# Layer 0's integer codes turned over as 16 bit halves: bf16 transposes and unsigned 16 bit copies out of PSUM

## Chip, cores, metric

The kernel runs on one core of a Trainium2 chip, as one launch. The metric is device time in microseconds; before the change it was 2154.37 us, the median of three runs (2153.43 to 2154.45). PE is the engine of the matmuls, DVE the vector engine, ACT the scalar engine, POOL the general one, SP the one that issues the loads.

## What is computed

The reference is a stack of four layers over x, 8 sequences ("elements") of 512 tokens and 256 features, with one conditioning row for each element. Layer 0, where the change lies, is a gated recurrent block and an MLP, all of whose linear maps are of one kind:

```
def _act_quant(x):      # each row to integers -128..127
    scale = 127.0 / clip(max(abs(x), axis=-1), 1e-05)
    return clip(round(x * scale), -128, 127) / scale
def _weight_quant(w):   # -1, 0, 1 times the mean magnitude
    scale = 1.0 / clip(mean(abs(w)), 1e-05)
    return clip(round(w * scale), -1, 1) / scale
def _bitlinear(x, w, nw):
    xn = x * rsqrt(mean(x^2) + 1e-08) * nw
    return _act_quant(xn) @ _weight_quant(w).T
```

For each element: `mx = layernorm(x) * (1 + scale) + shift`; i, f, g = three bitlinears of mx (256 to 256, each with its own norm weight); `i = silu(i) * (1 - sigmoid(f))`; a scan `h = f * h + i` over the tokens; `o = rmsnorm(h) * silu(g)`, a bitlinear of o (256 to 256), gated into x; then a layernorm again, a bitlinear 256 to 2048, `silu(gate) * y`, a bitlinear 1024 to 256, gated into x. Layers 1 (a style merge with a feed forward block), 2 (attention) and 3 (a state space block) follow; nothing of them is changed.

## The kernel before

The program has four parts: `setup` (layer 0's weights made ternary, the conditioning), `layers01` (layers 0 and 1 together), `layer2`, `layer3`. The change is in `layers01` alone. There x stays in SBUF as 8 elements of 4 tiles of 128 tokens. Every engine walks a hand-ordered table (`PE_TURN`, `DVE_TURN`, `ACT_TURN`, `POOL_TURN`) in its own order, once for each element; a row (stage, n, ahead) says which element, counted from the running one, the stage works on, so that several elements in different stages are under way at once. The order of an engine never changes; the engines wait on one another by semaphores.

The codes of a bitlinear take this way. ACT multiplies the rows by their scale and adds ROUND = 12582912 = 1.5 * 2^23 (stages `xq`, `xoq`, `xq2`, `hq`): this rounds to an integer and leaves it in the low mantissa bits of the f32 word. The matmul needs the features on the partitions, so PE turns each 128x128 block over against the f32 identity (`turn`, line 100 of the profile) into PSUM, as f32. DVE copies the turned blocks out of PSUM, subtracts ROUND and writes bf16, in which the integers are exact (stages `qT`, `qoT`, `qT2`, `qhT`: lines 1233, 1263, 1304, 1331). PE then multiplies by the ternary weights in bf16.

For one element: `xw` (three scaled copies of mx, 4 tiles of 6 blocks, 768 columns of PSUM over two banks a tile), `xo` (4 tiles of 2 blocks; its buffer is that of `th`), `mx2` (2 turns of 4 blocks) and `h` (8 turns of 4 blocks): 72 blocks. Two more kinds of transposes in layer 0, `fi` (from `th` and `si`) and `o` (from `si`), and layer 1's are real f32 values. Squares are summed by ACT (line 895) with an accumulator; the squared values themselves go to `junk` tiles that nobody reads.

Of the kernel before, what the change touches and what calls it, by code (L numbers as in the profile page):

```python
# [11 lines left out]
P = 128  # L12
ALU = mybir.AluOpType
ACT = mybir.ActivationFunctionType
AX = mybir.AxisListType
F32 = mybir.dt.float32
BF16 = mybir.dt.bfloat16

B, L, D = 8, 512, 256
T = L // P  # L20
KD = D // P
# [4 lines left out]

ROUND = 12582912.0


# [52 lines left out]
def tok(t):  # L82
    return slice(t * P, (t + 1) * P)
# [545 lines left out]
def layers01(nc, io, w, mean, ident, mod0, style1, x_res, x_loaded):  # L629

    H2 = io["c_harmonics"].shape[0]
    with ExitStack() as ctx:
        def sb(name, shape, dt=F32):
            return ctx.enter_context(nc.sbuf_tensor("l0_" + name, shape, dt))

        def sem(name):
            return nc.alloc_semaphore("l0_" + name)
# [43 lines left out]
        ifg_loaded, vectors_loaded, half_ready, halved = sem("ifg_loaded"), sem("vectors_loaded"), sem("half_ready"), sem("halved")  # L681
        norm_loaded, gate_loaded, mlp_loaded, style_loaded = (
# [43 lines left out]

        def two_banks(a):
            return psum[:, a:a + 2, :].rearrange("p a b -> p (a b)")

# [3 lines left out]
        with nc.Block() as block:  # L733
# [42 lines left out]
            def _(pool):  # L776
                gp = nc.gpsimd
# [110 lines left out]
            def _(act):  # L888
                ac = nc.scalar
# [7 lines left out]
                for stage, t, e in steps(ACT_TURN):  # L897
# [17 lines left out]
                    elif stage == "xq":  # L915

                        act.wait_ge(qs_ready.sem, qs_ready.at(e, 1))
                        for j in range(3):
                            last = ac.activation(xw[:, t, j, :], xw[:, t, j, :], ACT.Copy, bias=ROUND, scale=qs[e % 2][:, t, j:j + 1])
                        last.then_inc(xq_ready.sem, 1)  # L920
# [19 lines left out]
                    elif stage == "xoq":  # L940
                        act.wait_ge(qso_ready.sem, qso_ready.at(e, 1))
                        ac.activation(xo[:, t, :], xo[:, t, :], ACT.Copy, bias=ROUND, scale=qso[:, t:t + 1]).then_inc(xoq_ready.sem, 1)
                    elif stage == "ssq2":
# [4 lines left out]
                    elif stage == "xq2":  # L948
                        act.wait_ge(qs2_ready.sem, qs2_ready.at(e, 1))
                        ac.activation(mx2[:, t, :], mx2[:, t, :], ACT.Copy, bias=ROUND, scale=qs2[:, t:t + 1]).then_inc(xq2_ready.sem, 1)  # L950
                    elif stage == "silu":
# [9 lines left out]
                    elif stage == "hq":  # L961
                        act.wait_ge(qsh_ready.sem, qsh_ready.at(e, 1))
                        ac.activation(h[:, t, :], h[:, t, :], ACT.Copy, bias=ROUND, scale=qsh[:, t:t + 1]).then_inc(hq_ready.sem, 1)
                    elif stage == "setup":
# [51 lines left out]
            def _(pe):  # L1016
                for stage, t, e in steps(PE_TURN):
                    if stage == "xq":

                        pe.wait_ge(xq_ready.sem, xq_ready.at(e, t + 1))  # L1020
                        if t:
                            pe.wait_ge(qT_ready.sem, qT_ready.at(e, t))
                            pe.wait_ge(sg_ready.sem, sg_ready.at(e, t))
                        elif e:
                            pe.wait_ge(qoT_ready.sem, qoT_ready.at(e - 1, T))
                        for j in range(3 * KD):
                            last = turn(nc, two_banks(0)[:, tok(j)], xw[:, t, j // KD, tok(j % KD)], ident[:])
                        last.then_inc(turned.sem, 1)
# [26 lines left out]
                    elif stage == "xoq":  # L1055
# [3 lines left out]
                        for k in range(KD):  # L1059
                            last = turn(nc, psum[:, t % 2, tok(k)], xo[:, t, tok(k)], ident[:])  # L1060
                        last.then_inc(xo_turned.sem, 1)
# [5 lines left out]
                    elif stage == "xq2":  # L1067
# [6 lines left out]
                        for i in range(2):  # L1074
                            for k in range(KD):
                                last = turn(nc, psum[:, 4 + t, tok(KD * i + k)], mx2[:, 2 * t + i, tok(k)], ident[:])
                        last.then_inc(turned2.sem, 1)
# [7 lines left out]
                    elif stage == "hq":  # L1085
# [7 lines left out]
                        for k in range(T):  # L1093
                            last = turn(nc, psum[:, 4 + (3 * i + c) % 2, tok(k)], h[:, i, tok(c * T + k)], ident[:])
                        last.then_inc(h_turned.sem, 1)
# [82 lines left out]
            def _(dve):  # L1178
# [14 lines left out]
                for stage, t, e in steps(DVE_TURN):  # L1193
# [35 lines left out]
                    elif stage == "qT":  # L1229
                        dve.wait_ge(turned.sem, turned.at(e, t + 1))  # L1230
                        if e or t >= 2:
                            dve.wait_ge(y_ready.sem, y_ready.at(e, t - 1))
                        V.tensor_scalar(qT[:, t % 2, :, :].rearrange("p a n -> p (a n)"), two_banks(0)[:, 0:3 * D], ROUND, None,
                                        ALU.subtract).then_inc(qT_ready.sem, 1)
# [24 lines left out]
                    elif stage == "qoT":  # L1259
                        dve.wait_ge(xo_turned.sem, xo_turned.at(e, t + 1))  # L1260
                        if e or t >= 2:
                            dve.wait_ge(yo_ready.sem, yo_ready.at(e, t - 1))
                        V.tensor_scalar(qoT[:, t % 2, :, :].rearrange("p a n -> p (a n)"), psum[:, t % 2, 0:D], ROUND, None,
                                        ALU.subtract).then_inc(qoT_ready.sem, 1)
# [35 lines left out]
                    elif stage == "qT2":  # L1300
                        dve.wait_ge(turned2.sem, turned2.at(e, t + 1))
                        if e:
                            dve.wait_ge(up_ready.sem, up_ready.at(e - 1, 2 * T))
                        V.tensor_scalar(qT2[:, 2 * t:2 * t + 2, :, :].rearrange("p i a n -> p (i a n)"), psum[:, 4 + t, :], ROUND, None,
                                        ALU.subtract).then_inc(qT2_ready.sem, 1)
# [20 lines left out]
                    elif stage == "qhT":  # L1326
                        i, c = t // 2, t % 2
                        dve.wait_ge(h_turned.sem, h_turned.at(e, t + 1))
                        if e or i >= 2:
                            dve.wait_ge(y2_ready.sem, y2_ready.at(e, i - 1))  # L1330
                        V.tensor_scalar(qhT[:, i % 2, c * T:(c + 1) * T, :].rearrange("p a n -> p (a n)"), psum[:, 4 + (3 * i + c) % 2, :], ROUND, None,
                                        ALU.subtract).then_inc(qhT_ready.sem, 1)
# [1163 lines left out]
```

## Time and profile before

| | |
|---|---|
| median of 3 runs | 2154.37 us |
| profiled execution | 2156.48 us |
| its span, first to last instruction | 2154.3 us |
| mean granted clock of PE in the span | 0.913 |
| PE busy | 1839.9 us (85%), 8728 instructions |
| PE weight loads | 1104.3 us (51%) |
| DVE busy | 1328.7 us (62%) |
| ACT busy | 1121.0 us (52%) |
| POOL busy | 568.9 us (26%) |
| `layers01`, its first xl to the last f2 | about 92 to 813 us |

The span is of one profiled execution; busy times are sums of instructions, and those of PE overlap, since a matmul starts before the one ahead has ended. The granted clock is a share of PE's full clock, 2.4 GHz; 0.5 is its lower level, 1.2 GHz. Names in the rows leave out buffer numbers, so `l_mx` stands for mx and mx2, `l_small` for all the small vectors. Some matmul records can be missing from a trace.

### The profile page before, as it was taken

The page shows a single profiled execution, that of the slowest core. Times are in us where ns is not written, and L with a number is a line of the kernel's source. Part 1 is how long each engine was busy: PE and PEld are TensorE (multiplying, and loading weights), DVE is VectorE, ACT ScalarE, POOL GpSimd, SP SyncE. Part 2 cuts the span into 40 slices and gives each one's busy share as a digit, 9 for nine tenths or more (in the row PEclk, how much of TensorE's full clock was granted, in tenths as well). Part 3 has the DMA queues.
Part 4 walks back from the last instruction along what each step waited for, and adds up shares of the span by engine and source line. Part 5 has one row for each costly group of instructions (what it writes and reads, how often), then busy time and mean ns, then how long its engine had stood idle before and what let it go on. Part 6 is the DMA issues. An engine that isn't in the chain of part 4 may idle for free. (4 is left out here: it accounts for less than half of the span.)

```text
span 2154.3 us, 26196 instructions
## 1 busy us (share of the span) xinstructions
PE 1839.9 (85%) x8728; PEld 1104.3 (51%) x8744; DVE 1328.7 (62%) x2922; ACT 1121.0 (52%) x2127; POOL 568.9 (26%) x775
## 2 busy tenths in 40 slices
PE   2355779999999996589899999999999856899998
PEld 1133557677766674133454545454544445567666
DVE  5757698878876516668786868677774114332331
ACT  6556588888776521046756575666666400221221
POOL 0256565567445213000010101010101100323322
PEclk9656699999999997589999999999999977999999
DMA  9400000000000003220203021111200020000000
GB/s 373 127 33 8 18 18 1 18 18 14 1 13 11 3 1 98 52 59 5 63 3 64 7 59 26 40 34 32 53 14 3 6 96 1 3 18 10 20 10 20
DMA packets 88312, 78.20 MB, mean 36 GB/s; under 512 B 9969, under 2 KB 82123, under 8 KB 87923
## 3 DMA queue, kind: packets, MB, share of 16 engines
q1 hardware_dynamic: 88080, 76.50, 12.9%
q8 instruction: 71, 1.16, 0.2%
q14 instruction: 63, 0.51, 0.1%
q10 hardware_dynamic: 98, 0.03, 0.0%
HBM read 46.67 MB, written 4.27 MB: 24 GB/s over the span
## 5 line engine op out<-in xcount | busy, mean ns | idle before, releaser
L1896 DVE TENSOR_REDUCE l_small<-l_psum 128x1 f32<-128x512 f32 x512 | 329.5, 684 | 137.2 <-PE l_psum L1843 132.3
L1655 ACT ACTIVATE l_prob<-l_psum 128x512 f32<-128x512 f32 x512 | 286.4, 596 | 230.0 <-PE l_psum L1713 226.7
L1843 PE MATMUL l_psum<-l_kT,l_qT 96*128 96x512 bf16 x512 | 192.2, 412 | 27.1 <-DMA l_kT<-l_early 12.1
L1713 PE MATMUL l_psum<-l_qT,l_kT 99*128 99x512 bf16 x512 | 175.6, 388 | 16.0 <-ACT l_prob L1655 14.3
L1639 POOL TENSOR_TENSOR k_x_res<-k_x_res,l_add 128x256 f32<-128x256 f32 x32 | 23.3, 727 | 469.9 <-DVE l_add L1940 469.9
L1722 PE MATMUL l_psum<-l_prob,l_v 128*32 128x512 f32 x1024 | 138.1, 612 | 0.2
L1843 PEld LDWEIGHTS l_psum<-l_kT,l_qT 96*128 96x128 bf16 x512 | 49.6, 98 | 171.1 <-DVE l_small L1896 117.9
L1787 PE MATMUL l_psum<-l_w,l_gu 128*128 128x256 f32 x512 | 134.8, 392 | 0.7 <-ACT l_gu L1671 0.7
L94 PE MATMUL l_psum<-l_hT,l_w_f 128*128 128x512 f32 x256 | 120.0, 597 | 5.7 <-ACT l_gu L1013 5.7
L94 PE MATMUL l_psum<-l_hT,l_w 128*128 128x512 f32 x256 | 116.8, 606 | 8.6 <-ACT l_hT L2250 8.6
L94 PE MATMUL l_psum<-l_turned_over,l_w 128*128 128x512 f32 x256 | 120.5, 597 | 4.2 <-ACT l_gu L1671 4.2
L1173 PE MATMUL l_psum<-l_w_f,l_gu 128*128 128x256 f32 x512 | 118.0, 379 | 0.8 <-ACT l_gu L1013 0.8
L94 PE MATMUL l_psum<-l_w,l_gu 128*128 128x256 f32 x512 | 111.9, 379 | 0.8 <-ACT l_gu L2254 0.8
L1787 PEld LDWEIGHTS l_psum<-l_w,l_gu 128*128 128x128 f32 x512 | 97.4, 196 | 19.9 <-issue 2.4
L94 PEld LDWEIGHTS l_psum<-l_w,l_gu 128*128 128x128 f32 x512 | 96.7, 190 | 14.4 <-ACT l_gu L2254 1.6
L1713 PEld LDWEIGHTS l_psum<-l_qT,l_kT 99*128 99x128 bf16 x512 | 46.5, 98 | 108.3 <-ACT l_prob L1655 63.0
L1173 PEld LDWEIGHTS l_psum<-l_w_f,l_gu 128*128 128x128 f32 x512 | 94.5, 190 | 13.1 <-ACT l_gu L1013 1.6
L2254 ACT ACTIVATE l_gu<-l_psum,l_b 128x512 f32<-128x512 f32 x64 | 44.0, 688 | 96.2 <-PE l_psum L94 96.2
L2250 ACT ACTIVATE l_hT<-l_psum,l_shift,l_scale 128x512 f32<-128x512 f32 x16 | 11.7, 775 | 156.4 <-PE l_psum L100 156.4
L94 PE MATMUL l_psum<-l_w_qkv,l_xT 128*128 128x512 f32 (+1 forms) x256 | 90.5, 497 | 2.8 <-DVE l_xn L1958 1.9
L94 PEld LDWEIGHTS l_psum<-l_hT,l_w 128*128 128x128 f32 x256 | 48.4, 194 | 66.3 <-issue 55.6
L94 PE MATMUL l_psum<-k_t_wm,l_qT 128*128 128x512 bf16 x240 | 71.0, 404 | 13.1 <-DVE l_h L1311 7.3
(389 smaller groups left out, 3891.5 us busy)
## 6 DMA issues: line engine op xcount, KB each, us to landing
su_raw<-in_L_cond_wa SPq DMA_DIRECT2D x6, 1536.0 KB, 21.9
l_qT<-l_early SPq DMA_DIRECT2D x32, 192.0 KB, 3.6
l_kT<-l_early SPq DMA_DIRECT2D x32, 192.0 KB, 3.3
k_x_res<-in_x SPq DMA_DIRECT2D x1, 4096.0 KB
l_w<-in_L_cond_W SPq DMA_DIRECT2D x4, 1024.0 KB, 12.5
l_qT<-l_early SPq DMA_DIRECT2D x32, 128.0 KB, 3.1
l_kT<-l_early SPq DMA_DIRECT2D x32, 128.0 KB, 3.0
out<-k_x_res SPq DMA_DIRECT2D x8, 512.0 KB, 2.9
```

The costliest lines, as they stand in the source:

```text
L94: last = nc.tensor.matmul(out, w, m, start=(i == 0), stop=(i == len(pairs) - 1), **kw)
L1173: last = pe.matmul(psum[:, 6 + i % 2, 0:D], gu[:, f, tok(i)], w_f2[:, f, :], start=(f == 0), stop=(f == KF - 1))
L1639: pool.tensor_tensor(x_tile(e, n), x_tile(e, n), add2[:], ALU.add).then_inc(x_ready.sem, 1)
L1655: act.activation(prob[:, s % 2, j, :], psum[:, 2 + n % 2, :], ACT.Exp, scale=float(HD) ** -0.5).then_inc(exp_ready.sem, 1)
L1713: pe.matmul(psum[:, 2 + n % 2, :], kT[e % 2][:, head, tok(s % T)], qT[e % 2][:, head, :], start=True, stop=True).then_inc(st_ready.sem, 1)
L1722: last = pe.matmul(psum[j * BLOCK:(j + 1) * BLOCK, 4, :], v[e % 2][:, kt, at:at + BLOCK], prob[:, n % 2, j, :], start=(kt == 0), stop=(kt ...
L1787: last = pe.matmul(psum[:, mlp_bank(e, t), 0:D], gu[:, f, tok(t)], w_2[:, f, :], start=(f == 0), stop=(f == KF - 1))
L1843: pe.matmul(psum[:, n % 2, :], qT[e % 2][0:SROWS, n // T, tok(n % T)], kT[e % 2][0:SROWS, n // T, :], start=True, stop=True).then_inc(s_re ...
L1896: dve.tensor_reduce(mx[:, n % T, n // T:n // T + 1], psum[:, n % 2, :], AX.X, ALU.max).then_inc(max_ready.sem, 1)
L2250: act.activation(dst[:, k, :], psum[:, bank + k, :], ACT.Identity, scale=scale[:, k, bass.ds(nxt, 1)], bias=shift[:, k, bass.ds(nxt, 1)]). ...
L2254: act.activation(gu[:, n, :], psum[:, n % 2, :], ACT.Gelu_apprx_tanh, bias=b_1[:, n:n + 1]).then_inc(gu_ready.sem, 1)
```

## The change

ACT adds ROUND + CODE, with CODE = 16384, in place of ROUND. The word then is 0x4B400000 + 0x4000 + q, whose low half is 16384 + q, between 16256 and 16511. PE turns over only these low halves: `low` takes an f32 tile as bf16, two to a word, and picks the first of each pair, so the weights of the transpose are bf16 at a pitch of 4 bytes; the identity is a bf16 copy, `identb`, which POOL makes once. The output in PSUM is bf16, packed, so a tile of `xw` fills 1536 bytes of one bank and no longer two banks. DVE reads PSUM as unsigned 16 bit integers, subtracts CODE and writes bf16. PE waits for `identb` once, before the first turn. Five junk tiles of the squares become bf16; `junk_h` stays f32. Transposes of `fi`, `o` and layer 1 are not touched.

```
+CODE = 16384.0
-        junk = [sb(f"junk{i}", [P, D]) for i in range(5)]
+        junk = [sb(f"junk{i}", [P, D], BF16) for i in range(5)]
+        identb = sb("identb", [P, P], BF16)
+        def low(a):
+            return a.bitcast(BF16).rearrange("p (n a) -> p n a", a=2)[:, :, 0]
+        def halves(a):
+            return psum[:, a, :].bitcast(BF16)
+        def codes_in(a, n):
+            return psum[:, a, :].bitcast(U16)[:, 0:n]
 POOL, after its memsets and before its table:
+                gp.tensor_copy(identb[:], ident[:]).then_inc(identb_ready, 1)
 ACT xq; xoq, xq2 and hq alike:
-   ac.activation(xw[:, t, j, :], xw[:, t, j, :], ACT.Copy, bias=ROUND, scale=qs[e % 2][:, t, j:j + 1])
+   ac.activation(xw[:, t, j, :], xw[:, t, j, :], ACT.Copy, bias=ROUND + CODE, scale=qs[e % 2][:, t, j:j + 1])
 PE xq, t = 0, e = 0:
+                        else:
+                            pe.wait_ge(identb_ready, 1)
 PE xq; xoq, xq2 and hq alike:
-   last = turn(nc, two_banks(0)[:, tok(j)], xw[:, t, j // KD, tok(j % KD)], ident[:])
+   last = turn(nc, halves(0)[:, tok(j)], low(xw[:, t, j // KD, tok(j % KD)]), identb[:])
 DVE qT; qoT, qT2 and qhT alike:
-   V.tensor_scalar(qT[...], two_banks(0)[:, 0:3 * D], ROUND, None, ALU.subtract)
+   V.tensor_scalar(qT[...], codes_in(0, 3 * D), CODE, None, ALU.subtract)
```

## Rows read from the trace of the kernel before

**Rows 1.** Windows: start:end and length, busy us of each engine (instructions), clock
```profile
112.00:290.00 178.00, 109.84 (x486) 72.76 (x491) 129.60 (x249) 105.07 (x282) 105.99 (x143) 0.66 0.04 13
290.00:740.00 450.00, 429.80 (x2250) 308.65 (x2261) 352.75 (x729) 344.34 (x809) 250.93 (x343) 0.97 0.04 12
740.00:820.00 80.00, 69.96 (x267) 49.19 (x265) 17.43 (x43) 18.86 (x35) 9.34 (x15) 0.93 0.05 14
```

**Rows 2.** Waits of PE, 300 to 720 us: total us, times, longest
```profile
PE l_psum L94 <- ACT l_gu L1013: 5.7, 8, 0.9
PE l_psum L94 <- DVE l_h L1311: 2.4, 6, 0.5
PE l_psum L94 <- DVE l_qT L1233: 1.8, 1, 1.8
...
PE l_psum L94 <- DVE l_qhT L1331: 1.0, 2, 0.8
```

**Rows 3.** Groups of PE's transposes, 290 to 820 us: count, busy us, mean ns
```profile
L100 PE MATMUL l_psum<-k_ident,l_h 128*128 128x128 f32 x216 | 30.5, 274 | 0.8 <-DVE l_add L1337 0.7
...
L100 PE MATMUL l_psum<-k_ident,l_th 128*128 128x128 f32 x88 | 16.9, 273 | 1.4 <-ACT l_th L942 1.4
L100 PE MATMUL l_psum<-k_ident,l_xw 128*128 128x128 f32 x120 | 16.4, 273 | 1.7 <-ACT l_sg L927 1.7
...
L100 PE MATMUL l_psum<-k_ident,l_mx 128*128 128x128 f32 x48 | 7.0, 273 | 0.0
```

**Rows 4.** Timeline of PE: start us, us of the run, instruction, count
```profile
121.16 1.51 PE L100 MATMUL l_psum<-k_ident,l_xw 128*128 128x128 f32 x6 [1.39 <-ACT l_sg L927]
...
126.57 1.51 PE L100 MATMUL l_psum<-k_ident,l_xw 128*128 128x128 f32 x6 [1.39 <-ACT l_sg L927]
...
139.35 0.66 PE L100 MATMUL l_psum<-k_ident,l_th 128*128 128x128 f32 x2
...
438.65 1.89 PE L1173 MATMUL l_psum<-l_w_f,l_gu 128*128 128x256 f32 x8
439.52 0.81 PE L1173 MATMUL l_psum<-l_w_f,l_gu 128*128 128x256 f32 x3
...
442.99 0.82 PE L100 MATMUL l_psum<-k_ident,l_xw 128*128 128x128 f32 x6
```

**Rows 5.** Timeline of PE in the setup and in layer 2, bf16
```profile
27.99 0.89 PE L94 MATMUL su_t<-su_q,su_t_wa 128*128 128x8 bf16 x28
...
1552.19 0.61 PE L100 MATMUL l_psum<-l_identb,l_part 128*96 128x128 bf16 x8
```

**Rows 6.** Layer 2's tile part: count, ns min/median/max, first and last start
```profile
L100 PE MATMUL l_psum<-l_identb,l_part x512: 217/219/342, 848.2 to 1552.6; 128*96 128x128 bf16 x171
```

**Rows 7.** Groups of DVE's copies out of PSUM, whole span
```profile
L1331 DVE TENSOR_SCALAR l_qhT<-l_psum 128x512 bf16<-128x512 f32 x64 | 42.5, 683 | 5.7 <-PE l_psum L100 5.7
L1233 DVE TENSOR_SCALAR l_qT<-l_psum 128x768 bf16<-128x768 f32 x32 | 30.4, 949 | 10.7 <-PE l_psum L100 10.7
...
L1263 DVE TENSOR_SCALAR l_qoT<-l_psum 128x256 bf16<-128x256 f32 x32 | 13.3, 415 | 3.3 <-PE l_psum L100 3.1
L1912 DVE COPY k_max_rows<-l_psum 12x512 bf16<-12x512 bf16 x32 | 12.9, 405 | 11.8 <-PE l_psum L100 11.8
```

**Rows 8.** Waits between PE and DVE, 112 to 290 us
```profile
PE l_psum L94 <- DVE l_qT L1233: 9.0, 6, 2.6
...
DVE l_qT L1233 <- PE l_psum L100: 8.1, 6, 2.7
```

**Rows 9.** Groups of ACT that write values nobody reads, whole span
```profile
L895 ACT ACTIVATE l_junk<-l_mx 128x256 f32<-128x256 f32 x64 | 26.4, 413 | 16.6 <-POOL l_mx L844 9.1 <-POOL l_mx L807 6.5
...
L271 ACT ACTIVATE su_junk<-su_raw 128x256 bf16<-128x256 f32 x1 | 0.4, 417 | 0.0
```

**Rows 10.** Groups of POOL: layer 2's bf16 copy of the identity
```profile
L1617 POOL CAST l_identb<-k_ident 128x128 bf16<-128x128 f32 x1 | 0.3, 289 | 0.0
```

**Rows 11.** Timeline of POOL, its first work on x
```profile
90.71 0.20 POOL L796 TENSOR_SCALAR l_small<-l_small 128x4 f32<-128x4 f32 x1 [1.95 <-DVE l_small L1204]
```

**Rows 12.** Waits of ACT, 300 to 720 us
```profile
ACT l_h L956 <- PE l_psum L94: 22.7, 27, 4.8
```

More of the change, by code:

```diff
@@ L918, in _ @@
                         for j in range(3):
-                            last = ac.activation(xw[:, t, j, :], xw[:, t, j, :], ACT.Copy, bias=ROUND, scale=qs[e % 2][:, t, j:j + 1])
+                            last = ac.activation(xw[:, t, j, :], xw[:, t, j, :], ACT.Copy, bias=ROUND + CODE, scale=qs[e % 2][:, t, j:j + 1])
                         last.then_inc(xq_ready.sem, 1)
@@ L941, in _ @@
                         act.wait_ge(qso_ready.sem, qso_ready.at(e, 1))
-                        ac.activation(xo[:, t, :], xo[:, t, :], ACT.Copy, bias=ROUND, scale=qso[:, t:t + 1]).then_inc(xoq_ready.sem, 1)
+                        ac.activation(xo[:, t, :], xo[:, t, :], ACT.Copy, bias=ROUND + CODE, scale=qso[:, t:t + 1]).then_inc(xoq_ready.sem, 1)
                     elif stage == "ssq2":
@@ L949, in _ @@
                         act.wait_ge(qs2_ready.sem, qs2_ready.at(e, 1))
-                        ac.activation(mx2[:, t, :], mx2[:, t, :], ACT.Copy, bias=ROUND, scale=qs2[:, t:t + 1]).then_inc(xq2_ready.sem, 1)
+                        ac.activation(mx2[:, t, :], mx2[:, t, :], ACT.Copy, bias=ROUND + CODE, scale=qs2[:, t:t + 1]).then_inc(xq2_ready.sem, 1)
                     elif stage == "silu":
@@ L962, in _ @@
                         act.wait_ge(qsh_ready.sem, qsh_ready.at(e, 1))
-                        ac.activation(h[:, t, :], h[:, t, :], ACT.Copy, bias=ROUND, scale=qsh[:, t:t + 1]).then_inc(hq_ready.sem, 1)
+                        ac.activation(h[:, t, :], h[:, t, :], ACT.Copy, bias=ROUND + CODE, scale=qsh[:, t:t + 1]).then_inc(hq_ready.sem, 1)
                     elif stage == "setup":
@@ L1059, in _ @@
                         for k in range(KD):
-                            last = turn(nc, psum[:, t % 2, tok(k)], xo[:, t, tok(k)], ident[:])
+                            last = turn(nc, halves(t % 2)[:, tok(k)], low(xo[:, t, tok(k)]), identb[:])
                         last.then_inc(xo_turned.sem, 1)
@@ L1075, in _ @@
                             for k in range(KD):
-                                last = turn(nc, psum[:, 4 + t, tok(KD * i + k)], mx2[:, 2 * t + i, tok(k)], ident[:])
+                                last = turn(nc, halves(4 + t)[:, tok(KD * i + k)], low(mx2[:, 2 * t + i, tok(k)]), identb[:])
                         last.then_inc(turned2.sem, 1)
@@ L1093, in _ @@
                         for k in range(T):
-                            last = turn(nc, psum[:, 4 + (3 * i + c) % 2, tok(k)], h[:, i, tok(c * T + k)], ident[:])
+                            last = turn(nc, halves(4 + (3 * i + c) % 2)[:, tok(k)], low(h[:, i, tok(c * T + k)]), identb[:])
                         last.then_inc(h_turned.sem, 1)
@@ L1262, in _ @@
                             dve.wait_ge(yo_ready.sem, yo_ready.at(e, t - 1))
-                        V.tensor_scalar(qoT[:, t % 2, :, :].rearrange("p a n -> p (a n)"), psum[:, t % 2, 0:D], ROUND, None,
+                        V.tensor_scalar(qoT[:, t % 2, :, :].rearrange("p a n -> p (a n)"), codes_in(t % 2, D), CODE, None,
                                         ALU.subtract).then_inc(qoT_ready.sem, 1)
@@ L1303, in _ @@
                             dve.wait_ge(up_ready.sem, up_ready.at(e - 1, 2 * T))
-                        V.tensor_scalar(qT2[:, 2 * t:2 * t + 2, :, :].rearrange("p i a n -> p (i a n)"), psum[:, 4 + t, :], ROUND, None,
+                        V.tensor_scalar(qT2[:, 2 * t:2 * t + 2, :, :].rearrange("p i a n -> p (i a n)"), codes_in(4 + t, 2 * D), CODE, None,
                                         ALU.subtract).then_inc(qT2_ready.sem, 1)
@@ L1330, in _ @@
                             dve.wait_ge(y2_ready.sem, y2_ready.at(e, i - 1))
-                        V.tensor_scalar(qhT[:, i % 2, c * T:(c + 1) * T, :].rearrange("p a n -> p (a n)"), psum[:, 4 + (3 * i + c) % 2, :], ROUND, None,
+                        V.tensor_scalar(qhT[:, i % 2, c * T:(c + 1) * T, :].rearrange("p a n -> p (a n)"), codes_in(4 + (3 * i + c) % 2, T * P), CODE, None,
                                         ALU.subtract).then_inc(qhT_ready.sem, 1)
```

8 lines of the change are left out of this document (4 added, 4 removed).

## The prediction

> **What bounds the kernel now.** I read first the windows of the first section, from 112 to 820 us, because every edit lies in it and nothing else in the program is touched. The reader is to see two regimes [rows 1]. From 112 to 290 us the pipeline fills: PE is busy 110 of 178 us, its granted clock 0.66 on average, so between its two levels of 1.2 and 2.4 GHz; no engine is full, and chains that go from engine to engine set the pace. From 290 to 740 us PE is busy 430 of 450 us at a clock of 0.97; DVE has 353 and ACT 344. From 740 to 820 us PE is busy 70 of 80. Second, PE's own waits in the full part [rows 2]: the largest is 5.7 us in 420 us, on ACT's gelu. So from 290 us on PE's work is the time: what is taken from PE there comes off the end, nearly one for one. Third, how much of that work the edited transposes are [rows 3]: after 290 us 216 of `h`, 120 of `xw`, 48 of `mx2` (its row reads l_mx) and, of the 88 in the row of `th`, 48 of `xo`, which shares that buffer (the other 40 are `fi`'s, not edited: eight an element for five elements). That is 432 of the 576 edited ones (72 an element, eight elements), and 144 lie before 290 us.
>
> **The transposes.** An f32 transpose costs PE 0.11 us at the full clock: x6 in 0.82 us, one of them 0.273 [rows 3], so 0.55/5. At the low clock it is x6 in 1.51 and x2 in 0.66, so 0.85/4 = 0.21 [rows 4]. For a bf16 transpose the trace has layer 2's: x8 in 0.61 us, one of them 0.219, so 0.39/7 = 0.056 us [rows 5, 6]. Two things differ. Those weights are 96 columns wide, here they are 128; and they are packed, here each bf16 lies 4 bytes from the next. For the width the rows give a bound: scaled by 128/96 the pace would be at most 0.075 us. And 28 packed bf16 loads of 128 columns with 8 moving columns took 0.89 us [rows 5], at most 0.032 us each, so at full width the load isn't what limits and the 128 moving columns are: I take 0.056. For the 4-byte pitch no row exists: the low end is that of packed weights, the high end the pace of today's f32 load, 0.11, as it walks over the same bytes. I take the low end: f32 matmuls of 256 columns, x8 in 1.89 us and x3 in 0.81, are 1.08/5 = 0.216 apart [rows 4], so 128 f32 columns moved past the weights are 0.108 us; the moving identity alone accounts for the 0.11, and it becomes packed bf16.
> Saved: 0.053 us at the full clock, 432 times = 22.9 us after 290 us. At the low clock twice that, 0.107.
>
> The Trainium skill, "TensorE: Matmul & The Clock Gate", section "Weight-path perf modes", has the fast load of non-f32 weights of 128 columns work packed or strided. By that rule the sum stays at 22.9 us; without it and with a load at 0.11 it would be nothing. No row here shows the strided case.
>
> **The copies out of PSUM.** Today they read f32 and take 949 ns for 768 columns (`qT`, x32), 683 for 512 (`qhT`, x64; `qT2`, x16, is the same form) and 415 for 256 (`qoT`, x32) [rows 7]. That is (949-415)/512 = 1.04 ns a column and 148 ns fixed. A DVE copy of 512 bf16 out of PSUM into bf16 has a row: 405 ns [rows 7], which is 148 + 512 x 0.50: half the price of a column. It is a COPY on 12 partitions with bf16 in, not a subtraction with unsigned 16 bit integers in. Ends: nothing saved, or half of each column. I take half, the row it is nearest to: 0.40 us off each `qT`, 0.27 off each `qhT` and `qT2`, 0.13 off each `qoT`; in all 32 x 0.40 + 80 x 0.27 + 32 x 0.13 = 38.6 us of DVE. From 290 us on that is no time, since PE sets the end and waits only 1.8 + 1.0 us for such copies [rows 2]; it is cover, DVE's load falling from 353 to some 325 of 450.
> The trace's 405 ns and a rule disagree here: the Trainium skill, "VectorE: DVE Perf Modes", section "Rules for kernel authors", says to accept the 1x rate on what comes out of PSUM. By that rule the copies would keep 683 and 949 ns, the steady part would lose nothing, and the fill would give the lower value below.
>
> **The fill.** The first element's projection is a strict chain of transposes, `qT`, projection, silu, transposes again: the next tile's x6 starts 126.57-121.16 = 5.4 us later, all in series [rows 4]. Both halves of it shrink. PE waited 9.0 us in six waits for `qT`, each with a whole copy in it: 6 x 0.40 = 2.4 us less. DVE waited 8.1 us in six waits for these transposes at mostly the low clock: 6 x 6 x 0.107 = 3.9 us less [rows 8]. Together 6.3. The other 72 transposes of the fill (40 of `h`, 16 of `xo`, 16 of `mx2` [rows 3], by the same count) save 7.7 us of PE at the low clock, and their copies 10 x 0.27 + 4 x 0.27 + 8 x 0.13 = 4.8 us of DVE. About a third of that is on the path, as POOL and ACT stand between (POOL is busy 106 of the 178 us [rows 1]): 4. So 10 us. Ends: 4 (copies unchanged, half of the transposes' saving at the full clock on the path) and 17 (nearly all of it).
>
> **What costs nothing, and what its cover is.** The bias ROUND + CODE in place of ROUND is the same ACT instruction. The five junk tiles become bf16: ACT wrote 256 bf16 in 417 ns in setup and 413 ns in f32 here [rows 9], so 0 (ends -1 and +1 us over 188 squares). `junk_h` stays as it is. POOL gets one copy of the identity, 289 ns in layer 2 [rows 10], ahead of its list; its first work then waits 1.95 us for DVE's statistics [rows 11], so it is hidden; without cover 0.3 us. PE's new wait for it stands ahead of the first `xq` turn, more than 20 us later, behind it nothing that the copy could hold up. The 768 turned columns now fill one bank instead of one and a half; every wait stays, so no order changes.
>
> **What is late next.** An element takes 72 x 0.053 = 3.8 us less of PE in the full part. ACT was busy 344 of 450; with 23 us less it is 344 of 427, 81%. Its gelu already holds PE 5.7 us [rows 2] and its silu/`h` pair 2.4; I put 6 us of new waits there, against 3 us of old waits for copies that go: 3 us lost.
>
> **Sum.** -22.9 - 10 + 3 = -30 us. The profiled execution took 2156.48 us (span 2154.3), so 2126.5 by its own time; it lies 2.1 us above the median of the runs, 2154.37, and from that I forecast 2124.4 us.
>
> **Rivals.**
> (1) The list, not PE, takes over. Each engine's order is fixed; with PE 5% faster, the ACT and DVE steps between two PE stages come due earlier than they can be met. For it: ACT waits 22.7 us in the full part for PE's `gate` products [rows 12], and PE for what ACT and DVE make of them [rows 2], so that loop is tight. Against it: PE's waits are small now and DVE gets 39 us freer. Half of the 22.9 goes and the fill gives 6: -17, 2137 us.
> (2) The 4-byte pitch takes the load back to the f32 pace. For it: no row of a strided bf16 load. Against it: the moving operand accounts for the f32 price. Only the copies' gain in the fill is left, 4 to 5 us: 2150 us.
> (3) Slower than before: the same load, but costlier than an f32 one, since it fetches as many bytes for half the data and can't use what makes a packed one fast. The gain of the copies, 5 us, is spent once the pace is above 0.11 + 5/576 = 0.12 us. At 0.15 us it is 576 x 0.04 - 5 = +18: 2172 us. Against it: no transpose in the rows is slower than the f32 ones, and the element size alone has never cost, only saved [rows 4 to 6].
> (4) The clock. In the fill PE's clock falls to 1.2 GHz when PE pauses, and shorter transposes make PE idler. [...] If a tenth of the fill's 110 busy us fell from the high to the low level, it would cost 11 us, and in the full part, 97% at the high level, nothing: 2135 us.
> (5) The copies stay at today's price (no 16 bit gain): -22.9 - 5 + 4 = -24, 2130 us, inside the forecast's band.
>
> **How the numbers follow.** The forecast with its own band, 2112 to 2134, which takes in rival 5: 0.62. Rival 1: 0.18. Rival 4: 0.08. Rival 2: 0.06. Rival 3: 0.04. Better than the band (waits of the fill that go with it): 0.02. Ends for the range: 432 x 0.053 + 3 + 17 = 43 below, 2111; above, the pace of 0.075 with the fill at 5 and 6 us of new waits, 432 x 0.034 + 5 - 6 = 14 below, 2140. I take 2111 to 2141. A change within 0.2% (4.3 us) can't be told from none; that leaves faster 0.93, same 0.03, slower 0.04.
>
> **What would show it.** The transposes after the change: x6 of `xw` near 0.22 + 5 x 0.056 = 0.50 us at the full clock; 0.8 means rival 2, more rival 3. `qT` near 550 ns, `qhT` 410, `qoT` 280; unchanged means rival 5. PE still busy over 93% in the full part, and its waits for `l_gu` and `l_h` up by no more than 6 us; more is rival 1. The end of the first element's `qT` chain earlier by 3 to 4 us, and the granted clock of the fill at 0.6 or above; lower is rival 4. Everything after layer 1 keeps its length. The forecast is wrong if the pace is right and the section still ends less than 20 us earlier.

## The result, and the profile after

The changed kernel took 2133.39 us (median of four runs, 2133.16 to 2134.38) and the kernel before 2153.90 us on the same chip (four runs, 2153.01 to 2154.45): 20.5 us less, a ratio of 0.9906 with an interval of 0.9889 to 0.9923. The forecast was 2124.4, 30 us less. The number lies inside the range of 2111 to 2141, but nearer to rival 1 (2137) than to the forecast.

The profiled execution of the changed kernel took 2133.33 us, its span 2131.2. The prices of single instructions came out as forecast. PE's timeline after: start us, us, then the group with its count, and in brackets the idle time before it and what ended it.

```profile
120.74 0.80 PE L102 MATMUL l_psum<-l_identb,l_xw 128*128 128x128 bf16 x6 [1.38 <-ACT l_sg L939]
125.03 0.80 PE L102 MATMUL l_psum<-l_identb,l_xw 128*128 128x128 bf16 x6 [1.38 <-ACT l_sg L939]
...
417.05 0.61 PE L102 MATMUL l_psum<-l_identb,l_h 128*128 128x128 bf16 x8
417.50 1.13 PE L96 MATMUL l_psum<-l_w_merge,l_xT 128*128 128x256 f32 x4
...
435.32 0.49 PE L102 MATMUL l_psum<-l_identb,l_xw 128*128 128x128 bf16 x6 [0.32 <-ACT l_sg L939]
```

Six transposes take 0.49 us where they took 0.82, and 0.80 at the low clock where they took 1.51 [rows 4]. From the start of one to that of the next it is 0.056 and 0.107 us (eight in 0.61 us, one of them 0.219), as for layer 2's packed ones, though these codes lie 4 bytes apart. The copies, by the groups of DVE's work to 900 us (busy us, mean ns, then idle time before them):

```profile
L1345 DVE TENSOR_SCALAR l_qhT<-l_psum 128x512 bf16<-128x512 uint16 x64 | 25.4, 416 | 3.9 <-PE l_psum L102 3.9
L1247 DVE TENSOR_SCALAR l_qT<-l_psum 128x768 bf16<-128x768 uint16 x32 | 17.5, 548 | 7.3 <-PE l_psum L102 7.2
L1277 DVE TENSOR_SCALAR l_qoT<-l_psum 128x256 bf16<-128x256 uint16 x32 | 9.0, 280 | 2.6 <-PE l_psum L102 2.3
```

Forecast were 410, 550 and 280 ns; before it was 683, 949 and 415 [rows 7]. Now the windows of the section, as in [rows 1], and PE's waits from 300 to 700 us, as in [rows 2]:

```profile
112.00:290.00 178.00, 106.47 (x570) 67.21 (x575) 131.17 (x286) 114.36 (x308) 114.95 (x158) 0.68 0.05 13
290.00:740.00 450.00, 422.98 (x2225) 291.27 (x2236) 320.20 (x706) 338.39 (x791) 243.19 (x330) 0.96 0.04 12
```

```profile
PE l_psum L96 <- ACT l_gu L1025: 7.7, 9, 0.9
PE l_psum L96 <- DVE l_h L1325: 3.4, 9, 0.5
PE l_psum L102 <- ACT l_sg L939: 3.3, 10, 0.6
...
PE l_psum L102 <- DVE l_add L1351: 1.6, 6, 0.4
```

PE is still busy 94% of the full part, but it waits longer: 7.7 and 3.4 us for gelu and `h` (5.7 and 2.4 before), 3.3 us for ACT's `sg` (1.7 before, in a single wait) and 1.6 for `add2` (0.2 before).

Where the time came from is read from one DVE instruction that occurs once an element, the maximum over `mx2` (`amax2`), and from the last addition of the section (`x3`). Before:

```profile
176.36 1.22 DVE L1293 TENSOR_REDUCE l_small<-l_mx 128x4 f32<-128x1024 f32 x1
...
319.48 1.22 DVE L1293 TENSOR_REDUCE l_small<-l_mx 128x4 f32<-128x1024 f32 x1
392.23 1.22 DVE L1293 TENSOR_REDUCE l_small<-l_mx 128x4 f32<-128x1024 f32 x1
464.58 1.22 DVE L1293 TENSOR_REDUCE l_small<-l_mx 128x4 f32<-128x1024 f32 x1
...
678.92 1.22 DVE L1293 TENSOR_REDUCE l_small<-l_mx 128x4 f32<-128x1024 f32 x1
813.17 0.42 DVE L1424 TENSOR_TENSOR k_x_res<-l_psum,k_x_res 128x256 f32<-128x256 f32 x1 [3.03 <-PE l_psum L1173]
```

After:

```profile
171.26 1.22 DVE L1307 TENSOR_REDUCE l_small<-l_mx 128x4 f32<-128x1024 f32 x1
...
307.29 1.22 DVE L1307 TENSOR_REDUCE l_small<-l_mx 128x4 f32<-128x1024 f32 x1
379.37 1.22 DVE L1307 TENSOR_REDUCE l_small<-l_mx 128x4 f32<-128x1024 f32 x1
451.25 1.22 DVE L1307 TENSOR_REDUCE l_small<-l_mx 128x4 f32<-128x1024 f32 x1
...
659.80 1.22 DVE L1307 TENSOR_REDUCE l_small<-l_mx 128x4 f32<-128x1024 f32 x1
794.01 0.42 DVE L1438 TENSOR_TENSOR k_x_res<-l_psum,k_x_res 128x256 f32<-128x256 f32 x1 [3.03 <-PE l_psum L1187]
```

| up to `amax2` of element | 0 | 1 | 2 | 3 | 4 | 5 | 6 | 7 | last `x3` |
|---|---|---|---|---|---|---|---|---|---|
| gained, us | 5.1 | 8.3 | 12.2 | 12.9 | 13.3 | 16.5 | 18.5 | 19.1 | 19.2 |

By `amax2` of element 2 12.2 us have come, up to that of element 7 6.9 more, and behind it 0.1. The forecast parts the time at 290 us: 10 before and 22.9 - 3 = 19.9 from there on. Of the 432 edited transposes that it has there, 50 lie ahead of `amax2` of element 2, 342 between the two `amax2` and 40 behind. At 0.053 us each, that is a forecast of 12.7 us for the first stretch, 18.1 - 3 = 15.1 for the second and 2.1 for the third. The two periods after element 2 are 72.75 and 72.35 us before and 72.08 and 71.88 after, though PE's work in them fell from 70.4 to 67.7 us. The 23.1 us between the two profiled executions hold 4 more, which arise behind this section, where the program is the same; the medians don't show them.

### The profile page after: what moved, and what is told of

Its sections match the earlier page's. It is cut to its first block and busy times, and to the rows that moved or that the text cites. A ratio compares the mean times of both kernels' runs of the same rounds, so it can differ in the third digit from the quotient of the medians.

```text
span 2131.2 us, 26198 instructions
## 1 busy us (share of the span) xinstructions
PE 1810.8 (85%) x8728; PEld 1068.4 (50%) x8744; DVE 1293.4 (61%) x2922; ACT 1118.9 (53%) x2127; POOL 569.4 (27%) x776
## 3 DMA queue, kind: packets, MB, share of 16 engines
q1 hardware_dynamic: 88080, 76.50, 13.3%
```

## The experiments

All times are medians; each ratio is against runs of the kernel before on the same chip, where its median was 2154.1 (first four kernels), 2154.5 (next four), 2155.0 (next three) and 2154.6 us (last). Runs of one kernel scatter by some 3 us there. "The periods" are the two after element 2, read from `amax2` as above.

**The wait for `sg`.**

```
 if stage == "xq", t >= 1:
-    pe.wait_ge(sg_ready.sem, sg_ready.at(e, t))
```

The kernel before has this wait too, and there it cost 1.7 us once. The turned codes now fill the first bank alone, and `sg` is read out of another, so it orders nothing any more.

> The changed kernel without PE's wait for ACT's silu of g (sg_ready) ahead of the turns of xw for tiles 1 to 3. With f32 codes those turns ran into the second bank, which also holds g; the 768 halves of 2 bytes now lie in bank 0 alone, so nothing needs that wait any more. Theory A (the fixed lists: PE's saving was turned into waits, this one first): PE stood 1.1 us an element at it in the full part where it stood nothing before, and in the fill the turn and the copy are in series with projection and silu. The full part gives back some 5 us, the fill 1.4 us for each of 3 tiles of 2 to 3 elements, 8 us: 2120 us. Theory B (ACT's list binds the full part): the same time comes back as waits for gelu, and only the fill gains: 2127 us. Theory C (the wait is a symptom of no weight): 2132 to 2134 us.

2135.5 us, ratio 0.9913 (0.9898 to 0.9929): nothing gained. The waits for `sg` are gone, and PE waits 9.8 us for gelu and 2.2 for the silu of `h` instead of 7.7 and none in the list; the periods are 72.1 and 72.1. At `amax2` of element 2 this kernel is 1.5 us ahead of the changed one, at that of element 7 it is 2.0 behind. The wait was a symptom.

**Every edited transpose issued twice.**

```
+    turn(nc, halves(0)[:, tok(j)], low(xw[...]), identb[:])
     last = turn(nc, halves(0)[:, tok(j)], low(xw[...]), identb[:])
```

(and so for `xo`, `mx2` and `h`)

> The changed kernel with each of the 576 bf16 turns issued twice in a row, so that PE pays 0.11 us a block again as with f32, while DVE keeps its fast copies. If PE's work sets the time of the full part one for one, as predicted, 432 x 0.055 come back there and 144 x 0.055 to 0.11 in the fill: 2133 + 24 + 10 = 2167 us. Theory A (PE has slack against the other lists in the full part): the full part gives back the 7 us that it had gained and the fill about 8: 2148 us.

2148.0 us, ratio 0.9968 (0.9956 to 0.9979): 14.6 us above the changed kernel. PE has about the work of the kernel before again, and the copies are fast. This is the number of theory A, 19 us under that of one for one. The first period is 72.12 us all the same; the second is 73.58, and in it the granted clock is 0.95 and not 0.98 (last section). From `amax2` of element 2 to that of element 7 the kernel loses 7.9 us, where 19 us of PE's work (342 transposes of 0.056) were put back. In its periods of elements 3 and 4 that comes to 0.0 and 1.7 us over the changed kernel, in those of elements 5 to 7 to 6.1.

**The copies made slow again.**

```
-V.tensor_scalar(qT..., codes_in(0, 3 * D), CODE, None, ALU.subtract)
+V.tensor_tensor(qT..., codes_in(0, 3 * D), code[:, 0:1].to_broadcast([P, 3 * D]), ALU.subtract)
```

(all four kinds of copy)

> The changed kernel with the four kinds of copies out of PSUM as a subtraction of two tensors (the code constant in f32, one column read again and again), which should take what the f32 copies took: 949, 683 and 415 ns in place of 548, 416 and 280. Turns stay bf16. If the copies count only in the fill (as predicted): 5 us more, 2138 us, with the full part's period unchanged. If they are on a chain of the full part too, some 0.3 us for each of the 4 projections and more: 2145 us or above.

The view of the tile `qhT` shows the price of the kernel before (min/median/max ns):

```profile
L1344 DVE TENSOR_TENSOR l_qhT<-l_psum,l_small x64: 673/680/692, 203.7 to 715.7; 128x512 bf16<-128x512 uint16 x64
```

2140.7 us, ratio 0.9937 (0.9922 to 0.9952): the fast copies are worth some 7 us of the 20.5 (give or take the scatter of 3), against the 5 of rival 5. At `amax2` of element 2 it is 2.2 us behind the changed kernel, at that of element 7 it is 7.2.

**Less work for ACT.**

```
-squares(e, t, h[:, t, :], ssqh, ssqh_ready, junk_h)
+squares(e, t, h[:, t, 0:256], ssqh, ssqh_ready, junk_q)
```

It leaves out three quarters of the sum of squares over `h`.

> The changed kernel with ACT's sum of squares of h over 256 of its 1024 columns (leaves out three quarters of this sum): 0.64 us less of ACT for each tile, 2.6 us an element, nothing else touched. Theory B (ACT's list binds the full part): 1.5 to 2.6 us an element, 2133 - 14 = 2119 us. Theory A without ACT as the binding engine: at most 1 us an element and some in the fill: 2128 us or above.

2137.3 us, ratio 0.9924 (0.9906 to 0.9942), periods 73.1 and 73.5 (clock 0.98 and 0.95): no gain. ACT was busy 57.8 us in the first, 60.0 in the changed kernel's. ACT's load isn't what holds the pace.

**What goes round once an element.** At this point no engine's load explained the period, so I followed the releases back from one `amax2` to the one before, across the engines' timelines of the changed kernel. The rows below are those at which the chain changes engine, in order of time, ACT first:

```profile
381.58 1.71 ACT L962 ACTIVATE l_mx<-l_mx,l_small 128x256 f32<-128x256 f32 x4 [0.33 <-DVE l_small L1201]
387.23 0.69 ACT L968 ACTIVATE l_h<-l_psum,l_small 128x512 f32<-128x512 f32 x1
...
422.33 0.51 ACT L954 ACTIVATE l_th<-l_th,l_small 128x256 f32<-128x256 f32 x1 [1.68 <-DVE l_small L1201]
```

PE, DVE and POOL, each from its own timeline:

```profile
388.93 1.22 PE L96 MATMUL l_psum<-k_t_wm,l_qT 128*128 128x512 bf16 x4 [0.27 <-DVE l_h L1325]
389.99 1.94 PE L96 MATMUL l_psum<-l_small,l_g 128*128 128x1 f32 x16
391.79 2.02 PE L96 MATMUL l_psum<-l_small,l_z 128*128 128x1 f32 x16
```

```profile
404.80 0.75 DVE L1325 SCALAR_TENSOR_TENSOR l_h<-l_psum,l_small,l_h 128x512 f32<-128x512 f32 x1
...
406.59 0.74 DVE L1325 SCALAR_TENSOR_TENSOR l_h<-l_psum,l_small,l_h 128x512 f32<-128x512 f32 x1
...
418.61 0.75 DVE L1345 TENSOR_SCALAR l_qhT<-l_psum 128x512 bf16<-128x512 uint16 x2
...
422.14 0.16 DVE L1201 TENSOR_TENSOR l_small<-l_small 128x4 f32<-128x4 f32 x1
...
450.64 0.58 DVE L1304 TENSOR_TENSOR l_mx<-l_mx,l_n_m 128x256 f32<-128x256 f32 x1 [0.29 <-ACT l_junk L907]
```

```profile
423.32 0.19 POOL L793 TENSOR_SCALAR l_small<-l_small 128x4 f32<-128x4 f32 x1 [2.03 <-ACT l_junk L907]
...
436.53 0.79 POOL L808 TENSOR_SCALAR l_small<-l_small 128x4 f32<-128x4 f32 x1
...
449.28 0.79 POOL L856 TENSOR_TENSOR l_mx<-l_mx,l_mod_mlp 128x256 f32<-128x256 f32 x1
```

From `amax2` at 379.37 the scales go to ACT (codes of `mx2`, silu: 381.6 to 388), to PE (`gate` and `up`: 388.9 to 404.8, 16 us), to DVE (from the `h` at 404.8, the last but one, to the scales of `xo`, 17.5 us in which DVE never rests), through ACT's list (`ssq4` stands behind `xoq`, which waits for those scales) to POOL, which never rests from 423.3 to 452.4 us, over ACT's square and DVE's weighting of the last `mx2` tile, and so to the next `amax2` at 451.25. That is 71.88 us. On PE it has 16 us, in which PE runs none of the edited transposes and none of the `f2` products; of the edited ones only the eight of `mx2` are on the chain, just ahead of them. I call it the ring. Theory L from here on is this ring.

**A second helping for PE, after and before.**

```
-for f in range(t % 2 * T, t % 2 * T + T):
+for f in ((0, 2), (4, KF - 1))[t % 2]:
```

Half of layer 1's `f2` products are left out, 16 of 32 an element. Such an f32 product stands in the trace as two records 0.216 us apart (64 records in a period of the changed kernel, 32 here). So this takes off 6.9 us an element and not the 3.5 on which both expectations rest: 55 us in all, 35 of them between `amax2` of elements 2 and 7.

> The changed kernel with half of the f2 products of layer 1 left out (4 of 8 matmuls for each of the 32 tiles): 16 matmuls of 0.216 us an element, 3.5 us of PE, about as much as the change took away. A second helping of the same size. Theory L: in the elements where the loop decides (periods of 72.0 us) nothing comes of it, in the others and at the end of the section a part: 3 to 10 us off in all, 2124 to 2131 us. Theory P: 8 x 3.5 = 28 us less work, some of it hidden by waits, 18 to 26 us off, 2108 to 2116 us.

> The kernel before with the same half of the f2 products left out: PE gets the 3.5 us an element from another place than the transposes. Theory L: as the turns did in the full part, a third to a half of it: 8 to 16 us off, 2138 to 2146 us. Theory P: 18 to 26 us off, 2128 to 2136 us. If it is worth clearly more than the 7 us that the change brought in the full part, the transposes have a price of their own.

2114.6 us, ratio 0.9818 (0.9806 to 0.9831), and 2135.8 us, ratio 0.9916 (0.9902 to 0.9929). The totals, 18.8 us off the one and 18.7 off the other, lie in theory P's ranges and outside L's. But P's 18 to 26 us were worked out from 28 us less of work; from 55 it would be twice that, so P misses too. The periods decide, and they speak for L. These windows are one period of each kernel between two `amax2` (columns as in [rows 1]); in order the changed kernel, the one without half of `f2`, the one with each transpose twice, and the kernel before:

```profile
307.30:379.40 72.10, 67.79 (x375) 47.25 (x376) 58.33 (x131) 60.05 (x145) 46.70 (x65) 0.98 0.05 14
```

```profile
306.20:378.30 72.10, 62.23 (x343) 40.88 (x344) 58.62 (x131) 60.07 (x145) 46.68 (x65) 0.98 0.06 14
```

```profile
311.90:384.00 72.10, 70.47 (x447) 51.29 (x448) 58.12 (x130) 60.64 (x147) 46.28 (x66) 0.98 0.05 14
```

```profile
319.50:392.20 72.70, 70.62 (x376) 51.09 (x377) 62.73 (x130) 60.32 (x145) 46.51 (x65) 0.98 0.05 14
```

In the first three PE's work goes from 62.2 to 70.5 us and the period stays at 72.1. With half of `f2` gone PE idles 10 us in each, and at `amax2` of element 7 only 2.0 us have been gained, half of them in the fill, where 35 were taken off between the `amax2` of elements 2 and 7 (two of its five periods there have the clock of 0.95, one of the changed kernel's). The other 17.5 come behind it, where the last element leaves layer 0 and the ring is open. In the kernel before, the same cut brings 3.2 us between these two `amax2` and 15.3 behind them. PE's `f2` rows behind `amax2` of element 7, from 660 us to the section's end in the changed kernel and from 658 us in this one, are

```profile
L1187 PE MATMUL l_psum<-l_w_f,l_gu 128*128 128x256 f32 x192 | 43.5, 380 | 0.8 <-ACT l_gu L1025 0.8
```

```profile
L1187 PE MATMUL l_psum<-l_w_f,l_gu 128*128 128x256 f32 x96 | 22.7, 381 | 0.8 <-ACT l_gu L1025 0.8
```

20.8 us less work, 17.5 us gained: there, and not in the full part, PE pays nearly one for one. The edited transposes have hardly a share in that tail, 40 of the 576. Both theories' totals left this tail out of account.

Two stretches of the ring can be compared across the runs, in the first period, whose clock is 0.98 in all of these kernels (PE's busy time; from `amax2` to the last `h` of the element; from there to the maximum over `xo`; the period; in us):

| kernel | PE | to last `h` | to `amaxo` | period |
|---|---|---|---|---|
| changed, half of `f2` | 62.2 | 27.2 | 12.7 | 72.08 |
| changed | 67.8 | 27.2 | 12.7 | 72.08 |
| changed, transposes twice | 70.5 | 27.3 | 12.7 | 72.12 |
| before, half of `f2` | 65.0 | 27.3 | 13.2 | 72.58 |
| changed, slow copies | 68.1 | 27.2 | 13.2 | 72.48 |
| changed, `h` undone (next) | 69.5 | 27.2 | 13.2 | 72.61 |
| before | 70.6 | 27.3 | 13.2 | 72.75 |

The period sorts by the column of `amaxo` and not by PE's work. In that stretch DVE never rests and makes two copies of `h`'s codes (418.61 above, 0.75 us the two; 1.28 with the slow ones). These 0.53 us more go with a period that is 0.4 to 0.7 longer. With `h` undone it is 0.53 to the hundredth. So in these seven kernels the ring sets the pace, and what the change gained in it, 0.67 us in the first period, goes with these two copies, not with the transposes. The kernel with less work for ACT doesn't fit in: there the last `h` comes 28.2 us behind `amax2`, and why wasn't followed up.

**Only `h` undone.**

```
-ac.activation(h..., ACT.Copy, bias=ROUND + CODE, ...)
+ac.activation(h..., ACT.Copy, bias=ROUND, ...)
-turn(nc, halves(...)[:, tok(k)], low(h[...]), identb[:])
+turn(nc, psum[..., tok(k)], h[...], ident[:])
```

(and the copy reads f32 again)

> The changed kernel with the part of the change that concerns h undone: its 256 transposes move f32 again (0.11 us in place of 0.056), its codes carry no 16384 and its 64 copies read 512 f32 (683 ns in place of 416). 13.6 us of PE at the full clock and 17 us of DVE come back, 18 us of it on PE in all with the low clock. Theory P: the time rises by what PE gets, 12 to 18 us, 2145 to 2151 us. Theories L and M: h's transposes lie beside the loop in elements 3 and 4 and cost part of their time elsewhere: 3 to 8 us, 2136 to 2141 us. Then most of the gain comes from the chains of the fill, where xw's transposes and copies are.

2137.6 us, ratio 0.9926 (0.9909 to 0.9942): 4 us by the medians, where PE's bare work would cost 12 or more. In the profiled executions the section ends 7.1 us later than the changed kernel's, at the upper end of what L and M expected. `h` has 256 of the 576 transposes and 17 of the 39 us of saved copy time.

**Shortening the ring over POOL, after and before.**

```
-("x1", 1, 0), ("x2", 0, -1), ("x1", 2, 0), ("xb", 2, -3), ("xb", 3, -3), ("x1", 3, 0), ("mx", 3, 2), ("xb", 0, -2), ("x2", 1, -1), ("x2", 2, -1),
+("x1", 1, 0), ("x2", 0, -1), ("x1", 2, 0), ("x2", 1, -1), ("x1", 3, 0), ("x2", 2, -1),
```

(`mx` 3, `xb` 0 and 1 follow `rms2`, `xb` 2 and 3 follow `fac`)

> The changed kernel with POOL's list of the first section put in another order: four additions (xb) and one pair (mx of tile 3) that nothing waits for soon are taken out of the 29 us in which POOL never rests (423 to 452 us in the changed kernel's trace), so that root2 can start about 2.5 us sooner. Theory L (a loop): in the full part a chain of releases POOL, DVE, ACT, PE, DVE, POOL that comes round once an element and is 72.0 us long, only some 16 us of it on PE, sets the pace. Then the period falls by 1 to 2.5 us an element, until PE's own 67.7 us and its waits hold it: 6 to 14 us off, 2119 to 2128 us. Theory P (PE's work plus a few waits sets the pace): nothing on PE changes, so the same as the changed kernel within the chip's scatter, 2131 to 2137 us.

> The kernel before with the same new order of POOL's list. Theory L: there PE had 70.2 us of work in a period of 72.35, so there is little room under the loop: at most 1 us an element, 2 to 6 us off, 2148 to 2152 us, and the change is then worth more with the new order (24 to 28 us) than with the old one (20.5). Theory P: nothing, 2151 to 2156 us, and the change worth the same 20 us.

2136.5 us, ratio 0.9918 (0.9905 to 0.9931), and 2161.2 us, ratio 1.0034 (1.0022 to 1.0046). A miss for L's numbers twice over: no gain after, 7 us lost before; the first is as theory P has it. POOL's timeline of the first shows that the step did move up:

```profile
435.12 0.20 POOL L808 TENSOR_SCALAR l_small<-l_small 128x4 f32<-128x4 f32 x1 [1.03 <-DVE l_small L1298]
...
439.79 0.19 POOL L793 TENSOR_SCALAR l_small<-l_small 128x4 f32<-128x4 f32 x1 [1.22 <-ACT l_junk L907]
```

`root2` starts 1.4 us sooner, 0.7 of it against the `amax2` before it, and waits for its input now, but what it gained is given back 3 us later to a wait for ACT, which has hardly a pause between 425.8 and 449 us. The periods are 72.65 and 71.56. The stretch that was cut, from the last `h` to the next `amax2`, did shrink in the first of them, from 44.9 to 43.5 us, but the one from `amax2` to the last `h` grew from 27.2 to 29.1: PE now waits for the copies of `mx2`'s codes (6.8 us in six waits, 300 to 700 us, where it was 0.5).

The 7 us that the same order costs the kernel before lie all between `amax2` of elements 2 and 7. There three of the five periods (74.8, 75.1 and 73.9 us) have a clock of 0.95; in the kernel before it is one (74.1). That is part of the 7; the rest wasn't followed up.

**Shortening it between the `mx2` steps.**

```
-("root2", 0, 0), ("x2", 3, -1), ("sgn", 0, 1), ("root3", 0, -1), ("mx2", 0, 0), ("mx2", 1, 0), ("sgn", 1, 1), ("mx2", 2, 0), ...
+("root2", 0, 0), ("x2", 3, -1), ("root3", 0, -1), ("mx2", 0, 0), ("mx2", 1, 0), ("mx2", 2, 0), ("mx2", 3, 0),
+("rms2", 0, 0), ("sgn", 0, 1), ("sgn", 1, 1), ("xb", 1, -2), ...
```

The second kernel also puts ACT's `xl2` of tile 3 ahead of `xn` 0.

> The changed kernel with three steps of POOL's list put off that stood between its mx2 steps and that nothing waits for there: sgn of tiles 0 and 1 and xb of tile 1 now come after rms2, where POOL sat idle 7.9 us. In the changed kernel's trace the loop of 72 us goes over POOL from 440.7 to 450.1 us with POOL never resting (mx2 of four tiles, and between them two sgn of 0.73 us), then over DVE (amax2, scales), ACT (xq2, silu), PE (gate, up: 16 us), DVE (h, amaxh, scales: 17.5 us). Theory L (that loop sets the full part's pace, so what is taken off it comes off each period): 1.4 us an element in the four or five elements of which the loop holds the pace, if ACT's xl2 of tile 3 lets it: 4 to 8 us off, 2125 to 2130 us, periods of elements 3 and 4 at 70.5 to 71.2 instead of 72.0. Theory M (several loops of nearly this length, through ACT as well, each holds the pace alone; the run with POOL's other order is one sign): periods stay at 71.5 to 72.5, 2131 to 2136 us. Theory P (PE's work alone): no change either.

> The same, and in ACT's list xl2 of tile 3 stands ahead of the four xn, the load of the activation table and the gelu that it had waited behind (3.7 us). Theory L: both of what bounds mx2 of tile 3 move, so the loop gets 2 to 3 us shorter and PE's own 67.7 us with its waits comes next: 8 to 14 us off, 2119 to 2126 us. Theory M: xn and gelu come 0.6 us later, PE waits that much longer for gelu; periods stay within 0.7 us of 72: 2130 to 2137 us.

2137.0 us, ratio 0.9913 (0.9898 to 0.9928), and 2135.9 us, ratio 0.9916 (0.9901 to 0.9930); first periods 72.3 and 72.4. The second ones are 74.0 and 74.0, outside every range, and their clock is 0.95. The stretch from the last `h` to the next `amax2` shrank from 44.9 to 43.9 and 44.1 us in the first period, and the one from `amax2` to the last `h` grew from 27.2 to 28.3 in both. Theory M of these expectations is the nearest: its first periods are met, its totals too but for 1 us in the first. Beside the ring lie branches of nearly its length.

**Shortening what all branches seemed to share.**

```
-V.tensor_reduce(amaxh[:, t:t + 1], h[:, t, :], ...)
+V.tensor_reduce(amaxh[:, t:t + 1], h[:, t, 0:FF // 2], ...)
```

(`amaxo`, `amax` and `amax2` over half of their columns too, on top of the halved `f2`)

> The changed kernel with half of layer 1's f2 products left out, as in the run before of that name, and in layer 0 the four kinds of maximum (amaxh, amaxo, amax, amax2) taken over half of their columns. PE's work is untouched by this second cut, and in that run PE was busy only 62.2 of a period of 72.1 us. What the cut shortens is DVE's stretch from the last h to the scales of xo (17.5 us without a pause, about 404 to 422 us) and amax2, through which every one of the loops found so far goes: 2 x 0.55 us of amaxh, 0.6 of amaxo, 0.45 of amax and 0.6 of amax2, 2.8 us in a period. Theories L and M (a loop of releases through DVE, POOL, ACT and 16 us of PE sets the period, with side branches of nearly its length): the part that all branches share gets shorter, so the periods of elements 3 and 4 fall from 72.0 to 69.2 to 70.5 us, and the time from 2114.6 to 2098 to 2108 us. If the branches that don't pass these reductions hold the period, it stays at 71.5 to 72 and the loop isn't this one. Theory P: the maxima lie beside PE's work and are worth nothing: 2112 to 2117 us.

2109.7 us, ratio 0.9797 (0.9783 to 0.9811): 5 us less than without it, not 7 to 17, and the periods are 73.5 (clock 0.95) and 71.2 (0.98). At the same clock the second is 0.65 us shorter than without the cut, of 2.8 taken out. DVE is through earlier and then waits:

```profile
419.47 0.17 DVE L1197 TENSOR_TENSOR l_small<-l_small 128x4 f32<-128x4 f32 x1 [0.94 <-POOL l_small L845]
```

The scales of `xo` need POOL's `fac`, which hangs on ACT's sums over `u`: a second branch beside DVE's stretch, less than a microsecond shorter than it. That PE's work doesn't set the periods of elements 3 and 4 is shown, and that a stretch of the ring which gets longer makes the period longer. The other way round it isn't: three places were shortened, and each time most or all of it came back elsewhere. Which steps would have to get shorter together for the period to fall stays open. No version that does the whole work beat the changed kernel.

## Why the prediction was right and wrong

- *The pace of the transposes, the 4-byte pitch.* Right to the third digit, 0.056 and 0.107 us; rivals 2 and 3 are out. The product of 256 columns that the prediction sets beside them is one of the two records of an f32 product, which doesn't change the price of a pass. The low bound came from packed bf16 rows and the high one from f32 rows; the choice of the low one, because the moving identity alone accounts for f32's 0.11, was borne out.
- *The copies.* Right in ns. Their worth, 7 us by the slow copies, is a little above rival 5's 5. The rule of the Trainium skill that the prediction sets against its row ("VectorE: DVE Perf Modes", section "Rules for kernel authors"), by which they would have stayed at 683 and 949 ns, doesn't hold for these 16 bit integers out of PSUM.
- *The fill.* Right. 12.2 us against 10, or against 12.7 with the transposes between 290 us and `amax2` of element 2. The first element's projection chain repeats every 4.29 us instead of 5.41 (120.74, 125.03 above), and its end came 3.8 us earlier, as forecast (3 to 4). The clock there is 0.68, not under 0.6: rival 4 is out.
- *"So from 290 us on PE's work is the time: what is taken from PE there comes off the end, nearly one for one."* This is the step that failed. It read a load (430 of 450 us) as the cause of the pace. The period was 72.4 to 72.7 us with PE busy 70.4, and with fast copies a ring of releases through all four engines takes 72.1 us whatever PE has to do, between 62 and 70.5 us. Only 0.5 to 0.7 us a period came while the ring held, about what two copies in it gave; elements 5 to 7, where it is looser and the doubled transposes cost about half of their work (6.1 of 11 us), gave 5.8 us, and of that 3.2 in one whose period of before was lengthened by the clock as well (74.1 us at a mean of 0.95, last section).
- *"I put 6 us of new waits there."* The place was right in part (gelu and `h` up by 3 us), the size wrong: 15.1 us were due between the two `amax2` and 6.9 came. The prediction's own signs of rival 1, PE under 93% or these waits up by more than 6 us, didn't show, and yet not half of what was due came. A small wait isn't a small claim on the time: PE's 1.4 us a period for gelu and `h` (8.1 us in 420, [rows 2]) was the hint that it was being paced.
- *3.8 us of PE less in an element.* PE's busy time fell by 2.8 (70.4 to 67.7). Part of the rest stands in the rows: an f32 product right behind bf16 transposes takes 1.13 us for four instead of the usual 1.03, so some of what the transposes gave up goes to the next one's start; for those of `w_merge` and `f2` it is 0.5 us in one period (4.1 to 4.4 and 15.0 to 15.2).
- *The sum.* The stretch up to `amax2` of element 2 is right within 0.5 us, the next gave 8 less and the tail 2 less. By its own closing test (pace right and the section less than 20 us earlier) the forecast's reasoning is wrong, by 0.8 us. That the time still lies in the range is owed to its width of 30 us and not to the reasoning. Rival 1, the fixed lists, is what happened in the full part; it had 0.18. The doubled transposes (7.9 us of 19 there), the undoing of `h` (4 us of a bare 13.6) and the second helping show it.

## What to carry to other kernels

In a software pipeline of fixed lists, an engine at 97% isn't yet the bound. Measure the period between two occurrences of one instruction, follow the releases back from the one to the other, and count how much of that chain lies on the engine that you relieve: here 16 of 72 us. Then let two runs differ in that engine's work alone and see whether the period moves. Price the fill, the full part and the tail apart, since a microsecond of PE was worth 0.84 in the tail (17.5 of 20.8) and 0.03 to 0.4 in the full part (1 of 35 with half of `f2` gone, 7.9 of 19 with the transposes twice). And expect that shortening one step of such a ring lays bare a branch of nearly its length.

## What the runs showed of the hardware

- A transpose of bf16 codes that lie 4 bytes apart costs what layer 2's packed ones cost, 0.056 us for 128 x 128 at the full clock and 0.107 at the low one.
- A subtraction on unsigned 16 bit integers out of PSUM into bf16 takes half the time a column of one on f32 (416 against 683 ns for 512). As a subtraction of two tensors, the second of them one f32 column read again and again, it is lost: 680 ns.
- Of periods of equal work, some are 1.2 to 2 us longer, and these have a mean granted clock of 0.95 instead of 0.98, so more of them at the lower level, 1.2 GHz. Two successive periods of the kernel with `h` undone, and one of the kernel before:

```profile
308.20:380.80 72.60, 69.53 (x377) 48.75 (x376) 60.53 (x131) 60.06 (x145) 46.72 (x64) 0.98 0.05 14
380.80:454.80 74.00, 70.93 (x377) 49.98 (x376) 59.24 (x126) 59.97 (x145) 46.48 (x65) 0.95 0.07 14
```

```profile
464.60:538.70 74.10, 72.39 (x376) 52.50 (x377) 61.38 (x123) 60.41 (x145) 45.17 (x61) 0.95 0.03 10
```

- Where the clock falls is nearly the same in every period from element 2 on, of every kernel: 12 to 16 us behind `amax2`, during or right behind the 32 products of one column each on PE (389.99 to 393.8 above), which lie on PE's part of the ring. Two windows of the changed kernel:

```profile
389.80:393.60 3.80, 3.80 (x34) 3.62 (x33) 0.51 (x1) 0.82 (x2) 1.31 (x2) 0.99 0.00 0
393.60:396.80 3.20, 2.98 (x12) 1.91 (x13) 1.96 (x5) 1.20 (x3) 2.49 (x2) 0.50 0.00 0
```

  In the periods with 0.95 it stays at the low level for twice as long; with the transposes twice, the slow copies and `h` undone the last `h` then comes some 1.7 us later in the second period than in the first, and the period is 1.2 to 1.5 us longer. One or two such periods more or less may be most of the scatter of these runs; that was not tested.
